# State-space slots: plain fp32 output projection, and the scaled token tile divided between VectorE and GpSimd

## The chip, the core and the metric

One core of a Trainium2 chip runs the whole program. The time is device time of one execution in microseconds (us). The engines are TensorE (PE in the profile, with its weight loads as PEld), VectorE (DVE), ScalarE (ACT), GpSimd (POOL) and SyncE (SP), which here only issues DMAs. They run side by side and wait for one another on semaphores alone.

## What is computed

Two layers on x of shape 2 x 2048 x 256. The first is gated linear attention plus a feed-forward net and a mixture of 14 experts; the second is a state-space block (48 heads of 64 features, state 128) plus a mixture of 16 experts. The change is in the state-space block, whose reference, cut short, is:

```python
proj = _rms(x, norm_w) @ in_proj_w.T
z, xc, B, C, dt = split(proj)
xc = silu(conv_b + sum(conv_w[k] * xp[:, :, k:k + s] for k in range(4)))
dt, A = softplus(dt + dt_bias), -exp(A_log)
def step(h, ins):                       # for each head
    h = exp(A * dt_t) * h + B_t[:, None] * x_t[None, :]
    return h, einsum('np,n->p', h, C_t) + D * x_t
y = _rms(scan(step), inner_norm_w) * silu(z)
out = x + y @ out_proj_w.T
```

## The kernel before

`program` runs stages one after the other: `layer0` (first layer, without its experts), `experts`, `front` (what the second layer needs ahead), `experts1` and `ssm`. The change touches `ssm` and, for the weights that `ssm` reads, `layer0`.

**`ssm`.** Time is cut into G = 8 steps of 512 tokens (4 for each sequence). The 3072 inner features are cut into NCT = 24 tiles of 128, two heads each. A slot g is one tile in one step; N = 192 of them. The state of each tile goes from step to step in `chain`. Each engine runs its own list over the same beats `k`, and works in beat k on slots k to k - 4, so that up to five slots are under way:

- PE: `project(k)` (inputs to x and z, twelve matmuls of split operands), `scores(k-1)`, `update(k-1)` (what the tokens add to the state), `from_state(k-2)`, sometimes `row_turned` (an expert row of the second sequence, slots 6 to 37) and `mean_square`, then `project_out(k-4)` and `turn(k)`, four transposes of x.
- ACT: `convolve`, `output_high(k-4)`, `gate`, `differences`, `tanh`, `square(k-3)`, `decays` and `tokens(k)`, which copies the turned x out of PSUM into `x_tok`.
- POOL: `decayed(k-1)` (two products, tile `mm`), `output_low(k-4)`, `outputs(k-3)` (tiles `y` and `yz`), `squares(k-3)` (`y2`), and, in half of the slots, one small `edge` operation for the start of the convolution.
- DVE: `to_end(k-1)` (tile `xd`, the turned x times its weight up to the end of the chunk), `convolve`, `gate`, `silu`, `scan(k-1)`, `own_tokens(k-1)`, `state_part(k-2)`.

A "split" operand is a pair of tiles, high and low, whose sum is the fp32 value. `mm3` (L60) makes one product of two such pairs in three matmuls; their records have the lines L64, L65 and L66. `yz` is split by `output_high` on ACT (`y_hi`, L2661) and `output_low` on POOL (`y_lo`, L2712), and `project_out` waits for `y_lo`. The weights `wo` come split from HBM, 256 KB a slot.

Order is set by semaphores: `done(engine, name, g)` waits until event `name` has happened for slot g. Once a step, behind its last tile, `mean_square` on PE, `inverse_norm` on ACT (which loads two activation tables) and `evacuate` on DVE finish the step.

**`layer0`.** The weights of `ssm` are split there, tile by tile, between other work: a DMA brings a tile, DVE scales its last 256 columns (`scale_out`, event `s_wo`), ACT copies 768 columns to the high part (L796), POOL subtracts to the low part (L960), and DMAs carry both to `ssm_wi_split` and `ssm_wo_split`.

Of the kernel before, what the change touches and what calls it, by code (L numbers as in the profile page):

```python
# [5 lines left out]
F32 = mybir.dt.float32  # L6
# [7 lines left out]
P = 128  # L14
B, T, D = 2, 2048, 256
KD = D // P
TS = 512
# [82 lines left out]
def program(nc, xT, table, gla_w, gla_wo, wbc, moe0, ffn0, moe1, mamba, a_dram, outT):  # L100
    ctx = ExitStack()
    with ctx:
# [26 lines left out]
        wi_dram = nc.dram_tensor("ssm_wi_split", (NCT, P, 2 * MP_IN), F32, kind="Internal").ap()  # L129
        wo_dram = nc.dram_tensor("ssm_wo_split", (NCT, P, 2 * MP_OUT), F32, kind="Internal").ap()  # L130
        a_drams = (a_dram, nc.dram_tensor("a_scratch1", (HM, T), F32, kind="Internal").ap())
# [115 lines left out]
def layer0(nc, pool, bank, table, tab, vec_dram, xT, gla_w, gla_wo, ffn0, m_dram, ffn_dram, wi_dram, wo_dram, acc_dram, moe0, moe1, down_drams, rows_dram,  # L247
# [11 lines left out]
    with ExitStack() as own:  # L259
# [90 lines left out]
        def done(eng, name, g, per=1):  # L350

            if g >= 0:
                eng.wait_ge(ph[name], (g + 1) * per)
# [39 lines left out]
        with nc.Block(no_gpsimd_drain=True) as block:  # L393

            @block.sync
            def _(sp):
# [22 lines left out]
                def keep(n):  # L419

                    if n is None:
                        return
                    done(sp, "low", n)
                    if n + 1 < SPLITS:
                        fetch(n + 1)
                    if n < NT:
                        sp.dma_start(ffn_dram[n], s_out[:].bitcast(F32)).then_inc(ph["s_kept"], 16)
                    else:
                        parts = s_out[:].bitcast(F32).rearrange("p (h c) -> p h c", h=2)
                        sp.dma_start(wi_dram[n - NT].rearrange("p (h c) -> p h c", h=2), parts[:, :, 0:MP_IN]).then_inc(ph["s_kept"], 16)  # L430
                        sp.dma_start(wo_dram[n - NT].rearrange("p (h c) -> p h c", h=2), parts[:, :, MP_IN:MLP]).then_inc(ph["s_kept"], 16)

# [329 lines left out]
            def _(act):  # L762
# [26 lines left out]
                def high(n):  # L789
                    if n is None:  # L790
                        return
                    split_in(act, n)
                    split_kept(act, n - 1)
                    if n >= NT:
                        done(act, "s_wo", n - NT)
                    act.activation(s_out[:, 0:MLP], s_raw[:, 0:MLP], ACT.Copy).then_inc(ph["high"], 1)  # L796

# [133 lines left out]
            def _(pl):  # L931
# [24 lines left out]
                def low(n):  # L956
                    if n is None:
                        return
                    done(pl, "high", n)
                    pl.tensor_tensor(s_out[:, MLP:2 * MLP], s_raw[:, 0:MLP], s_out[:, 0:MLP].bitcast(F32), ALU.subtract).then_inc(ph["low"], 1)  # L960

# [1374 lines left out]
def ssm(nc, pool, bank, m_dram, wi_dram, wo_dram, a_drams, ea_drams, dec_dram, acc_dram, rows_out, f_dram, outT, st, vec_dram, swdge, tab, col):  # L2336
# [3 lines left out]
    with ExitStack() as own:  # L2340
# [6 lines left out]
        wi = sb("wi", [P, R, 2 * MP_IN], F32R)  # L2347
        wo = sb("wo", [P, R, 2 * MP_OUT], F32R)
        a_wide = sb("a_wide", [P, R, 2, TS])
# [15 lines left out]
        yz = sb("yz", [P, 2, TS])  # L2365
        y_hi, y_lo = sb("y_hi", [P, TS], F32R), sb("y_lo", [P, TS], F32R)
        y2, yr = sb("y2", [P, TS]), sb("yr", [P, TS])
# [40 lines left out]
        with nc.Block(no_gpsimd_drain=True) as block:  # L2408

            @block.sync  # L2410
            def _(sp):
# [17 lines left out]
                def weights_out(g):  # L2429
                    done(sp, "out", g - R)  # L2430
                    sp.dma_start(wo[:, g % R, :].bitcast(F32), wo_dram[g % NCT]).then_inc(ph[f"wo{g % R}"], 16)

# [78 lines left out]
            def _(pe):  # L2511
# [21 lines left out]
                def update(g):  # L2533
                    done(pe, "xd", g)
                    done(pe, "state", g - 1, NJ)
                    for j in range(NJ):
                        i = pe.matmul(bank[:, UPD, chunk(j)], b_tok[:, g // NCT * NJ + j, :], xd[:, j, :],  # L2537
                                      start=True, stop=True)
                    i.then_inc(ph["u"], 1)
# [17 lines left out]
                def project_out(g):  # L2557
                    t, s = g % NCT, g // NCT
                    done(pe, "y_lo", g)
                    landed(pe, "wo", g)  # L2560
                    if t == 0:
                        done(pe, "evac", s - 1)
                    for m in range(KD):
                        a = m * P
                        i = mm3(pe, bank[:, OUT + m, :], (wo[:, g % R, a:a + P], wo[:, g % R, MP_OUT + a:MP_OUT + a + P]),
                                (y_hi[:], y_lo[:]), t == 0, t == LAST)
                    i.then_inc(ph["out"], 1)
# [46 lines left out]
            def _(act):  # L2614
# [42 lines left out]

                def output_high(g):
                    done(act, "yz", g)
                    done(act, "out", g - 1)  # L2660
                    act.activation(y_hi[:], yz[:, g % 2], ACT.Copy).then_inc(ph["y_hi"], 1)  # L2661

                def tokens(g):
                    done(act, "xt", g)
                    done(act, "intra", g - 1)
                    act.activation(x_tok[:].rearrange("p j c -> p (j c)"), bank[:, XT, :], ACT.Copy).then_inc(ph["x_tok"], 1)

# [10 lines left out]
                for k in BEATS:  # L2678
                    if has(k):
                        convolve(k)  # L2680
                    if has(k - 4):
                        output_high(k - 4)
                    if has(k):
                        gate(k)
                        differences(k, 0)
                        tanh(k)
                    if has(k - 3):
                        square(k - 3)
                    if has(k):
                        differences(k, 1)  # L2690
                    e = k - 4
                    if has(e) and e % NCT == LAST:
                        inverse_norm(e // NCT)
                    if has(k):
                        decays(k)
                        tokens(k)

            @block.gpsimd
            def _(pl):
# [8 lines left out]

                def output_low(g):
                    done(pl, "y_hi", g)  # L2710
                    done(pl, "out", g - 1)
                    pl.tensor_tensor(y_lo[:], yz[:, g % 2], y_hi[:].bitcast(F32), ALU.subtract).then_inc(ph["y_lo"], 1)  # L2712

                def outputs(g):
# [6 lines left out]
                    done(pl, "zs", g)  # L2721
                    done(pl, "y_lo", g - 2)
                    pl.tensor_tensor(yz[:, g % 2], y[:], zs[:, g % NS], ALU.mult).then_inc(ph["yz"], 1)  # L2723
# [39 lines left out]
                for k in BEATS:  # L2763
                    if has(k - 1):
                        decayed(k - 1)
                    if has(k - 4):
                        output_low(k - 4)
                    if has(k - 3):
# [9 lines left out]
            def _(dve):  # L2778
# [68 lines left out]
                def to_end(g):  # L2847
                    s, t = g // NCT, g % NCT
                    done(dve, "x_tok", g)
                    done(dve, "u", g - 1)  # L2850
                    dve.tensor_tensor(xd[:].rearrange("p j (h c) -> p j h c", h=2),
                                      bank[:, XT, :].rearrange("p (j h c) -> p j h c", j=NJ, h=2),
                                      w_tok[:, s * NJ:(s + 1) * NJ, 2 * t:2 * t + 2].unsqueeze(3)
                                      .broadcast_to([P, NJ, 2, PH]), ALU.mult).then_inc(ph["xd"], 1)

# [134 lines left out]
```

## Time and profile before

| | |
|---|---|
| time, median of 3 runs | 3035.02 us (3034.8 to 3040.43) |
| profiled execution, span | 3067.1 us, nothing of it lies outside the span |
| PE busy | 2711.5 us, 88% |
| DVE busy | 2384.6 us, 78% |
| ACT busy | 2110.9 us, 69% |
| POOL busy | 1973.4 us, 64% |
| `ssm` | from about 1517 us to the end |

How to read it: the shares are averages over five stages. In the second half of the span, which is `ssm`, each of the four engines is busy for nine tenths or more of nearly every slice; in the first half none but PE is. A matmul's record begins when it starts and ends when its last result is out, so neighbours overlap: what one occupies is the distance to the next start. In the timelines a row stands for several equal instructions in succession (x4), and its second number is from the first start to the last end.

### The profile page before, as it was taken

The numbers are of one execution on the slowest core, as the hardware profiler recorded it, in microseconds if no ns is written. First come the engines' busy times: TensorE is split into PE (matmuls) and PEld (weight loads), VectorE is DVE, ScalarE is ACT, GpSimd is POOL, SyncE is SP. The second block draws the span as 40 slices with busy tenths as digits, with TensorE's granted clock in tenths as the row PEclk, the third lists the DMA queues.
The fourth block names the chain that finished last, engine by engine and source line by source line (L and its number), as shares of the span: only waits on it lengthen the run. The fifth ranks groups of instructions, "written<-read, shape, count | busy, mean of one in ns | idle before, by whom it ended". The sixth has DMA issues, their size and how long they took to land.

```text
span 3067.1 us, 58582 instructions
## 1 busy us (share of the span) xinstructions
PE 2711.5 (88%) x17318; PEld 2120.1 (69%) x17318; DVE 2384.6 (78%) x5972; ACT 2110.9 (69%) x4670; POOL 1973.4 (64%) x1697
## 2 busy tenths in 40 slices
PE   4799999998569888379799999999999999999997
PEld 2466666665469765267588788787887878878786
DVE  3466666666377589558599999998899999999896
ACT  4444454443255466346599999998999999999996
POOL 3322222214424214555399999998999999999998
PEclk7799999997889899689899999999999999999999
DMA  6355445455766544446777776767666666676673
GB/s 168 94 176 170 168 165 185 149 195 168 238 178 199 168 154 151 157 128 199 230 240 237 236 237 205 220 204 220 219 206 217 205 210 216 205 224 199 203 218 113
DMA packets 320436, 588.35 MB, mean 192 GB/s; under 512 B 47888, under 2 KB 138800, under 8 KB 319632
## 3 DMA queue, kind: packets, MB, share of 16 engines
q1 hardware_dynamic: 305776, 545.07, 57.6%
q0 software_dynamic: 14352, 39.54, 3.5%
q8 instruction: 149, 2.44, 0.3%
q14 instruction: 159, 1.30, 0.1%
HBM read 464.44 MB, written 124.17 MB: 192 GB/s over the span
## 4 chain that ended last, share of the span: by engine, by line
POOL 34%; issue 10%; ACT 3%; DVE 1%; PE 1%; DMA 1%; POOLq 1%; SPq 0%; ACTq 0%; DVEq 0%
POOL mm L2706 8%; POOL y L2719 7%; POOL yz L2723 7%; POOL y L2733 6%; POOL y_lo L2712 6%; ACT mt L2636 1%; DVE cv L2789 1%; DMA wi<-ssm_wi_split 1%; POOLq L2382 1%; ACT ys L2650 0%; ACT mt L2656 0%; DVE bank L2860 0%; ACT L2671 0%; POOL first L2748 0%; PE bank L64 0%
## 5 line engine op out<-in xcount | busy, mean ns | idle before, releaser
L2706 POOL TENSOR_TENSOR mm<-mt,cb 128x512 f32<-128x512 f32 x384 | 490.2, 1299 | 56.9 <-ACT mt L2656 54.9
L2636 ACT ACTIVATE mt<-a_wide,a_tok 128x128 f32<-128x128 f32 x1536 | 487.1, 389 | 3.5 <-POOL mm L2706 2.5
L2789 DVE SCALAR_TENSOR_TENSOR cv<-bank,taps,cv 128x509 f32<-128x509 f32 (+2 forms) x576 | 429.3, 745 | 13.6
L64 PE MATMUL bank<-f,wi 128*128 128x512 f32 x768 | 322.4, 420 | 14.7 <-DMA wi<-ssm_wi_split 14.6
L65 PE MATMUL bank<-f,wi 128*128 128x512 f32 x768 | 305.7, 398 | 0.0
L66 PE MATMUL bank<-f,wi 128*128 128x512 f32 x768 | 305.7, 398 | 0.0
L2723 POOL TENSOR_TENSOR yz<-y,zs 128x512 f32<-128x512 f32 x192 | 249.2, 1298 | 15.0
L2712 POOL TENSOR_TENSOR y_lo<-yz,y_hi 128x512 fp32r<-128x512 f32 x192 | 246.2, 1282 | 8.4 <-ACT y_hi L2661 6.5
L2719 POOL TENSOR_TENSOR y<-t 128x512 f32<-128x512 f32 x192 | 246.0, 1281 | 0.0
L2529 PE MATMUL bank<-mm,x_tok 128*64 128x128 f32 x3072 | 226.4, 283 | 13.1 <-POOL mm L2706 13.1
L2733 POOL TENSOR_TENSOR y<-y,ys 128x512 f32<-128x512 f32 x184 | 237.6, 1292 | 0.1
L2529 PEld LDWEIGHTS bank<-mm,x_tok 128*64 128x64 f32 x3072 | 161.4, 136 | 102.9 <-issue 68.1
L2656 ACT ACTIVATE mt<-mt 128x512 f32<-128x512 f32 x384 | 221.4, 624 | 5.9
L2537 PE MATMUL bank<-xd,b_tok 128*128 128x128 f32 x1536 | 223.4, 289 | 0.0
L2537 PEld LDWEIGHTS bank<-xd,b_tok 128*128 128x128 f32 x1536 | 186.7, 192 | 33.1 <-issue 33.1
L960 POOL TENSOR_TENSOR l_s_out<-l_s_raw,l_s_out 128x768 fp32r<-128x768 f32 x33 | 60.5, 1834 | 205.3 <-ACT l_s_out L796 205.3
L2831 DVE SCALAR_TENSOR_TENSOR part<-part,dec,bank 128x64 f32<-128x64 f32 x768 | 181.6, 278 | 13.6
L64 PEld LDWEIGHTS bank<-f,wi 128*128 128x128 f32 x768 | 146.0, 190 | 42.5 <-DMA wi<-ssm_wi_split 15.4
L64 PE MATMUL bank<-y_hi,wo 128*128 128x512 f32 x384 | 171.7, 447 | 3.5 <-POOL y_lo L2712 3.4
L1406 POOL DMA_INDIRECT expert_scratch<-ex_y,ex_home x77 | 73.7, 957 | 150.8 <-ACT ex_y L1495 147.8
L66 PEld LDWEIGHTS bank<-f,wi 128*128 128x128 f32 x768 | 145.6, 190 | 35.8
L65 PEld LDWEIGHTS bank<-f,wi 128*128 128x128 f32 x768 | 146.4, 191 | 26.6
(476 smaller groups left out, 8067.5 us busy)
## 6 DMA issues: line engine op xcount, KB each, us to landing
wi<-ssm_wi_split SPq DMA_DIRECT2D x192, 512.0 KB
a_wide<-a_scratch SPq DMA_DIRECT2D x192, 512.0 KB
l_fw<-ffn_split SPq DMA_DIRECT2D x72, 768.0 KB
ea<-ea_scratch SPq DMA_DIRECT2D x384, 128.0 KB
wo<-ssm_wo_split SPq DMA_DIRECT2D x192, 256.0 KB, 4.1
sorted_scratch<-ex_zeros SPq DMA_DIRECT2D x96, 130.5 KB
ssm_wi_split<-l_s_out SPq DMA_DIRECT2D x24, 512.0 KB
ey_x<-sorted_scratch SPq DMA_DIRECT2D x94, 130.5 KB
```

The lines of the kernel that those rows point to most:

```text
L64: pe.matmul(out, wh, xh, start=first, stop=False)
L65: pe.matmul(out, wh, xl, start=False, stop=False)
L66: return pe.matmul(out, wl, xh, start=False, stop=last)
L2529: i = pe.matmul(bank[h * PH:(h + 1) * PH, INTRA, chunk(j)], x_tok[:, j, h * PH:(h + 1) * PH], mm[:, h, chunk(j)], start=True, stop=True)
L2537: i = pe.matmul(bank[:, UPD, chunk(j)], b_tok[:, g // NCT * NJ + j, :], xd[:, j, :], start=True, stop=True)
L2636: i = act.activation(mt[:, h, chunk(j)], a_wide[:, g % R, h, chunk(j)], ACT.Relu, bias=a_tok[:, s * NJ + j, 2 * t + h:2 * t + h + 1], scal ...
L2706: pl.tensor_tensor(mm[:, :, ts], mt[:, :, ts], cb[:, js, :].rearrange("p j t -> p (j t)") .unsqueeze(1).broadcast_to([P, 2, TS // 2]), ALU ...
L2712: pl.tensor_tensor(y_lo[:], yz[:, g % 2], y_hi[:].bitcast(F32), ALU.subtract).then_inc(ph["y_lo"], 1)
L2719: pl.tensor_tensor(y[:], t1[:], t2[:, g % 2], ALU.add).then_inc(ph["y"], 1)
L2723: pl.tensor_tensor(yz[:, g % 2], y[:], zs[:, g % NS], ALU.mult).then_inc(ph["yz"], 1)
L2733: pl.tensor_tensor(y2[:], y2[:], ys[:], ALU.add).then_inc(ph["y2"], 1)
L2789: dve.scalar_tensor_tensor(cv[:, a:TS], bank[:, X, 0:TS - a], taps[:, t, k:k + 1], cv[:, a:TS], ALU.mult, ALU.add).then_inc(ph["tap"], 1)
```

## The change

Three things. The output projection takes `yz` and `wo` as plain fp32 instead of split: `y_hi`, `y_lo`, `output_high` and `output_low` are gone, and each `mm3` becomes one matmul. The tile `xd` is made in two halves: VectorE makes that of the first head, GpSimd (`second_to_end`) that of the second from `x_tok`, right behind `decayed`; `update` waits for both. In `layer0` the 256 columns of `wo` are only copied, not split.

```diff
@@ layer0, sync
-                        parts = s_out[:].bitcast(F32).rearrange("p (h c) -> p h c", h=2)
-                        sp.dma_start(wi_dram[n - NT].rearrange("p (h c) -> p h c", h=2), parts[:, :, 0:MP_IN]).then_inc(ph["s_kept"], 16)
-                        sp.dma_start(wo_dram[n - NT].rearrange("p (h c) -> p h c", h=2), parts[:, :, MP_IN:MLP]).then_inc(ph["s_kept"], 16)
+                        parts = s_out[:].bitcast(F32)
+                        sp.dma_start(wi_dram[n - NT].rearrange("p (h c) -> p h c", h=2),
+                                     parts.rearrange("p (h c) -> p h c", h=2)[:, :, 0:MP_IN]).then_inc(ph["s_kept"], 16)
+                        sp.dma_start(wo_dram[n - NT], parts[:, MP_IN:MLP]).then_inc(ph["s_kept"], 16)
@@ layer0, scalar
-                    if n >= NT:
-                        done(act, "s_wo", n - NT)
-                    act.activation(s_out[:, 0:MLP], s_raw[:, 0:MLP], ACT.Copy).then_inc(ph["high"], 1)
+                    if n < NT:
+                        act.activation(s_out[:, 0:MLP], s_raw[:, 0:MLP], ACT.Copy).then_inc(ph["high"], 1)
+                        return
+                    act.activation(s_out[:, 0:MP_IN], s_raw[:, 0:MP_IN], ACT.Copy)
+                    done(act, "s_wo", n - NT)
+                    act.activation(s_out[:, MP_IN:MLP].bitcast(F32), s_raw[:, MP_IN:MLP], ACT.Copy).then_inc(ph["high"], 1)
@@ layer0, gpsimd
-                    pl.tensor_tensor(s_out[:, MLP:2 * MLP], s_raw[:, 0:MLP], s_out[:, 0:MLP].bitcast(F32), ALU.subtract).then_inc(ph["low"], 1)
+                    w = MLP if n < NT else MP_IN
+                    pl.tensor_tensor(s_out[:, MLP:MLP + w], s_raw[:, 0:w], s_out[:, 0:w].bitcast(F32), ALU.subtract).then_inc(ph["low"], 1)
@@ ssm
-        wo = sb("wo", [P, R, 2 * MP_OUT], F32R)
+        wo = sb("wo", [P, R, MP_OUT])
-        y_hi, y_lo = sb("y_hi", [P, TS], F32R), sb("y_lo", [P, TS], F32R)
@@ ssm, tensor
                 def update(g):
                     done(pe, "xd", g)
+                    done(pe, "xd1", g)
                     done(pe, "state", g - 1, NJ)
                 def project_out(g):
                     t, s = g % NCT, g // NCT
-                    done(pe, "y_lo", g)
+                    done(pe, "yz", g)
                     landed(pe, "wo", g)
                     if t == 0:
                         done(pe, "evac", s - 1)
                     for m in range(KD):
-                        a = m * P
-                        i = mm3(pe, bank[:, OUT + m, :], (wo[:, g % R, a:a + P], wo[:, g % R, MP_OUT + a:MP_OUT + a + P]),
-                                (y_hi[:], y_lo[:]), t == 0, t == LAST)
+                        i = pe.matmul(bank[:, OUT + m, :], wo[:, g % R, m * P:(m + 1) * P], yz[:, g % 2], start=t == 0, stop=t == LAST)
@@ ssm, scalar
-                def output_high(g):
-                    done(act, "yz", g)
-                    done(act, "out", g - 1)
-                    act.activation(y_hi[:], yz[:, g % 2], ACT.Copy).then_inc(ph["y_hi"], 1)
                 def tokens(g):
                     done(act, "xt", g)
                     done(act, "intra", g - 1)
+                    done(act, "xd1", g - 1)
@@ ssm, gpsimd
-                def output_low(g):
-                    done(pl, "y_hi", g)
-                    done(pl, "out", g - 1)
-                    pl.tensor_tensor(y_lo[:], yz[:, g % 2], y_hi[:].bitcast(F32), ALU.subtract).then_inc(ph["y_lo"], 1)
+                def second_to_end(g):
+                    s, t = g // NCT, g % NCT
+                    done(pl, "x_tok", g)
+                    done(pl, "u", g - 1)
+                    pl.tensor_tensor(xd[:, :, PH:P], x_tok[:, :, PH:P],
+                                     w_tok[:, s * NJ:(s + 1) * NJ, 2 * t + 1:2 * t + 2]
+                                     .broadcast_to([P, NJ, PH]), ALU.mult).then_inc(ph["xd1"], 1)
-                    done(pl, "y_lo", g - 2)
+                    done(pl, "out", g - 2)
@@ ssm, vector
-                    dve.tensor_tensor(xd[:].rearrange("p j (h c) -> p j h c", h=2),
-                                      bank[:, XT, :].rearrange("p (j h c) -> p j h c", j=NJ, h=2),
-                                      w_tok[:, s * NJ:(s + 1) * NJ, 2 * t:2 * t + 2].unsqueeze(3)
-                                      .broadcast_to([P, NJ, 2, PH]), ALU.mult).then_inc(ph["xd"], 1)
+                    dve.tensor_tensor(xd[:, :, 0:PH], bank[:, XT, :].rearrange("p (j c) -> p j c", j=NJ)[:, :, 0:PH],
+                                      w_tok[:, s * NJ:(s + 1) * NJ, 2 * t:2 * t + 1]
+                                      .broadcast_to([P, NJ, PH]), ALU.mult).then_inc(ph["xd"], 1)
```

## Rows read from the trace of the kernel before

**Rows 1.** The profile's page, its first line.
```profile
span 3067.1 us, 58582 instructions
```

**Rows 2.** Busy time: stretch, PE, PEld, DVE, ACT, POOL, then granted clock, DMA.
```profile
2249.00:2289.00 40.00, 40.00 (x289) 33.03 (x286) 36.72 (x78) 37.21 (x90) 39.53 (x32) 1.00 0.66 205
```

**Rows 3.** The page's chain that ended last, by line: share of the span.
```profile
POOL mm L2706 8%; POOL y L2719 7%; POOL yz L2723 7%; POOL y L2733 6%; POOL y_lo L2712 6%; ACT mt L2636 1%; DVE cv L2789 1%; DMA wi<-ssm_wi_split 1%; POOLq L2382 1%; ACT ys L2650 0%; ACT mt L2656 0%; DVE bank L2860 0%; ACT L2671 0%; POOL first L2748 0%; PE bank L64 0%
```

**Rows 4.** Timeline of POOL, a regular slot: start us, us, engine, line, operation.
```profile
2271.68 1.29 POOL L2712 TENSOR_TENSOR y_lo<-yz,y_hi 128x512 fp32r<-128x512 f32 x1
2272.91 1.29 POOL L2719 TENSOR_TENSOR y<-t 128x512 f32<-128x512 f32 x1
...
2279.35 1.28 POOL L2712 TENSOR_TENSOR y_lo<-yz,y_hi 128x512 fp32r<-128x512 f32 x1
```

**Rows 5.** Timeline of PE, the same slot, from turn (L2584) to turn.
```profile
2267.99 0.60 PE L2584 MATMUL bank<-tab,xs 128*128 128x128 f32 x4
...
2271.32 1.12 PE L2529 MATMUL bank<-mm,x_tok 128*64 128x128 f32 x16
2272.36 1.16 PE L2537 MATMUL bank<-xd,b_tok 128*128 128x128 f32 x8
2273.36 0.39 PE L2546 MATMUL bank<-c_feat,chain 128*128 128x128 f32 x2
...
2274.17 0.48 PE L64 MATMUL bank<-y_hi,wo 128*128 128x512 f32 x1
2274.49 0.39 PE L65 MATMUL bank<-y_lo,wo 128*128 128x512 f32 x1
...
2275.42 0.39 PE L66 MATMUL bank<-y_hi,wo 128*128 128x512 f32 x1
2275.65 0.60 PE L2584 MATMUL bank<-tab,xs 128*128 128x128 f32 x4
```

**Rows 6.** Timelines of PE and POOL in slots with an expert row.
```profile
1714.18 0.60 PE L2584 MATMUL bank<-tab,xs 128*128 128x128 f32 x4
...
1722.04 0.60 PE L2584 MATMUL bank<-tab,xs 128*128 128x128 f32 x4
...
1722.40 0.48 PE L64 MATMUL bank<-f,wi 128*128 128x512 f32 x1
...
1722.94 2.59 POOL L2706 TENSOR_TENSOR mm<-mt,cb 128x512 f32<-128x512 f32 x2
...
1726.40 1.16 PE L2537 MATMUL bank<-xd,b_tok 128*128 128x128 f32 x8
```

**Rows 7.** Timeline of PE in `front`: four plain fp32 instructions and what follows.
```profile
1095.80 1.88 PE L1690 MATMUL bank<-fr_acc,tab 128*128 128x512 f32 x4
1097.52 1.04 PE L1716 MATMUL bank<-tab,fr_xn 128*128 128x128 f32 x8
```

**Rows 8.** Timeline of POOL, one edge operation.
```profile
2404.83 0.23 POOL L2748 TENSOR_TENSOR first<-halo,taps 128x12 f32<-128x12 f32 x1
```

**Rows 9.** Line 796, the copy in `layer0`: ns min/median/max; what its engine waited for.
```profile
L796 ACT ACTIVATE l_s_out<-l_s_raw x33: 827/847/852, 20.7 to 664.4; 128x768 fp32r<-128x768 f32 x33
...
  DVE l_s_raw L1219: 73.5, 24
```

**Rows 10.** Timeline of POOL: four of the 25 starts of y in 24 slots.
```profile
2249.92 1.26 POOL L2719 TENSOR_TENSOR y<-t 128x512 f32<-128x512 f32 x1
...
2303.86 1.28 POOL L2719 TENSOR_TENSOR y<-t 128x512 f32<-128x512 f32 x1
...
2331.13 1.33 POOL L2719 TENSOR_TENSOR y<-t 128x512 f32<-128x512 f32 x1
...
2440.11 1.28 POOL L2719 TENSOR_TENSOR y<-t 128x512 f32<-128x512 f32 x1
```

**Rows 11.** Timelines of PE and POOL where a step ends: idle before, releaser.
```profile
2309.12 0.63 PE L2584 MATMUL bank<-tab,xs 128*128 128x128 f32 x4 [0.94 <-ACT yr L2671]
...
2311.59 2.52 POOL L2706 TENSOR_TENSOR mm<-mt,cb 128x512 f32<-128x512 f32 x2 [3.84 <-ACT mt L2656]
```

More of the change, by code:

```diff
@@ L129, in program @@
         wi_dram = nc.dram_tensor("ssm_wi_split", (NCT, P, 2 * MP_IN), F32, kind="Internal").ap()
-        wo_dram = nc.dram_tensor("ssm_wo_split", (NCT, P, 2 * MP_OUT), F32, kind="Internal").ap()
+        wo_dram = nc.dram_tensor("ssm_wo_scaled", (NCT, P, MP_OUT), F32, kind="Internal").ap()
         a_drams = (a_dram, nc.dram_tensor("a_scratch1", (HM, T), F32, kind="Internal").ap())
@@ L2430, in weights_out @@
                     done(sp, "out", g - R)
-                    sp.dma_start(wo[:, g % R, :].bitcast(F32), wo_dram[g % NCT]).then_inc(ph[f"wo{g % R}"], 16)
+                    sp.dma_start(wo[:, g % R, :], wo_dram[g % NCT]).then_inc(ph[f"wo{g % R}"], 16)
                 def inputs(s):
@@ L2680, in _ @@
                         convolve(k)
-                    if has(k - 4):
-                        output_high(k - 4)
                     if has(k):
@@ L2765, in _ @@
                         decayed(k - 1)
-                    if has(k - 4):
-                        output_low(k - 4)
+                        second_to_end(k - 1)
                     if has(k - 3):
```

## The prediction

> **What bounds the kernel now.** I read the page's span first [rows 1], then asked in which stage the change lives. Its loop runs 192 times (8 steps of 512 tokens, 24 pairs of heads each); I call one turn of it a slot. The slots fill about half of the span, so 0.1 us a slot is 19 us, 0.6%. Next comes the table of busy time in a stretch without any special slot [rows 2]: over 40 us PE is busy for 40.00, POOL for 39.53, ACT for 37.21, DVE for 36.72, at a granted clock of 1.00. The chain of waits names POOL lines nearly alone [rows 3]. Reading only that would say that POOL is the bound; the reader should see that PE is just as full, and ask which of the two has the higher floor.
>
> POOL in one regular slot [rows 4]: y_lo, y, yz, y2 and the two halves of mm, back to back, and the next y_lo starts 7.67 us after this one. y_lo takes 1.23 of it, start to start.
>
> PE in the same slot [rows 5]: from turn to turn 7.66 us. Three products with split operands follow one another every (2275.42 - 2274.49) / 4 = 0.2325 us. The pieces: turn and input projection 3.33 us (2267.99 to 2271.32), scores 1.04, update 1.00, from_state 0.81, output projection 1.48. There is no hole in it.
>
> Is 7.66 PE's own floor, or does it follow POOL? The slots that also turn an expert row tell [rows 6]. There are 32 of them (row_turned, slots 6 to 37); PE gets two more transposes, POOL nothing. The period of one is 1722.04 - 1714.18 = 7.86 us, longer than the regular one by 0.20, and two transposes like the turn's four, which occupy 1722.40 - 1722.04 = 0.36 us, are worth 0.18. POOL has ended its mm there (1722.94 + 2.59 = 1725.53) well before PE is through the scores (1726.40). So PE does not follow POOL in this slot: its floor is 7.86 there and some 7.66 elsewhere. PE and POOL are tied within 0.02 us.
>
> **The change part by part.**
> *PE, output projection.* Removed: six matmuls with split operands, 6 x 0.2325 = 1.40 us. (The block spans 1.48 from its first start, but the first record begins 0.08 us before from_state has left the array: from_state's eight instructions take 0.81 there, while the eight of update take 1.00 with 0.1 of entry, so 0.08 belongs to it.) Added: two plain fp32 matmuls of 128x512, which are two instructions each. The same form at the same granted clock, right behind a stream of split products, stands in the stage ahead: four instructions, and the next work of PE starts 1097.52 - 1095.80 = 1.72 us later [rows 7]. So PE gets 1.72 - 1.40 = +0.32 us a slot; +0.24 if the 1.48 is taken instead. I take 0.32, because the 0.08 is made up elsewhere, and keep 0.24 for the low end. PE's slot: 7.66 + 0.32 = 7.98, or 8.18 with an expert row.
>
> Beside this stands a rule of the Trainium skill: "FP8 and Floating Point Precision", TensorE Precision Notes, gives true fp32 four passes through the array. Split products make three. By four passes at 0.2325 the block would take 8 x 0.2325 = 1.86 us, +0.46 a slot. The row disagrees with that: 0.43 us for an instruction is less than two such passes (0.465). The rule points the same way as the row and is a rival below.
>
> *POOL.* Removed: y_lo, 1.23 us. Added: xd1, a 128x256 product. No row has that size; bounds are the 128x12 product of the edge, 0.23 us [rows 8], and the 128x512 ones, 1.28 [rows 4]. Half-way in width lies 0.23 + (1.28 - 0.23) x 244 / 500 = 0.74, which I take. POOL's slot: 7.67 - 1.23 + 0.74 = 7.18 (6.67 to 7.72 from the bounds), and at most 0.2 more where an edge operation runs. All below 7.98: the gain is hidden behind PE.
>
> *ACT* loses y_hi, *DVE* half of xd. Both have slack already, 37.21 and 36.72 of 40 [rows 2]; what they lose brings nothing. Nobody waits for them longer.
>
> *The added wait: update(k-1) on xd1(k-1).* Queued behind it on PE are from_state, the output projection, the turn and the next input projection. PE gets there 1726.40 - 1722.40 = 4.00 us after its input projection started. POOL, now earlier in the slot because it has nothing to catch up on, ended mm 3.13 us after the same moment in the PE-bound slot [rows 6]; plus 0.74 is 3.87. That holds by 0.13 us even without POOL moving forward; with a slot that is 0.32 us longer for PE, ACT and POOL gain that as well. Cost taken: nothing. If xd1 took 1.28, update would start up to 4.41 - 4.00 = 0.41 late without the shift, about 0.1 with it. The wait of the copy into x_tok for xd1 of the slot before, and of yz for the projection two back, end many microseconds before they are asked.
>
> *DMA.* wo comes as 128 KB instead of 256 KB a slot, and nobody waits for it now: nothing.
>
> *The split of the weights in the first layer* (24 tiles). ACT copies 768 columns in 0.85 us, and has waited 73.5 / 24 = 3.1 us before each for VectorE's scaling of the last 256 [rows 9]. Now 512 of them are copied within this wait and only 256 after it, so the tile is done some 0.5 us earlier; at most 24 x 0.5 = -12 us if all of it lay on the path, at worst +24 x 0.2 = +5 for one more instruction. PE is the fullest engine in that stage and hardly waits for these tiles; I take -2.
>
> **The sum.** One step without expert rows has 24 slots in 2440.11 - 2249.92 = 190.19 us [rows 10]. Three of them are special: around the mean square, POOL's y goes from 2303.86 to 2331.13, 27.27 us. In these PE stands idle for 0.94 us before a turn because it waits for ACT's logarithm, and POOL waits 3.84 for the exponentials [rows 11]. The longer projection of that slot disappears in the 0.94; of the other two one gets 0.32; the last, which waits on POOL now, I give 0.1: 27.7. The other 21 slots take (190.19 - 27.27) / 21 = 7.76 on average: POOL's edge operations make half of them longer than 7.67. PE's floor levels them all to 7.98, since POOL's 7.18 + 0.2 stays below it: 21 x 7.98 + 27.7 = 195.3, +5.1 us a step. The 160 slots without expert rows are 6.67 steps: +34. The 32 others get 0.32 each: +10. With the -2: +42 us. Against the profiled execution, 3067.1 us of span with nothing to add around it, that is 3109; the median of the runs is 32 us (1%) below the profiled one, and a difference of 42 scales by nothing that matters: 3035 + 42 = **3077 us**, +1.4%.
>
> **The rivals.**
> (a) *POOL alone sets the slot and PE's fullness is following* (the other side, faster). Then a regular slot goes from 7.76 to about 7.3, 160 x 0.46 = -74, about 2960 us; it decides if PE's 7.86 with an expert row were not a floor. For it: the chain names POOL. Against it: rows 6, and the 1.72 us of [rows 7]. 5%.
> (b) *No change*: half the 0.32 is made up, say by loads of weights that PE no longer waits for (four instead of six), and the edge slots hide the rest: within 6 us of 3035. 4%.
> (c) *update waits for xd1.* If GpSimd's strided product with a broadcast weight costs as much as a full one, PE loses 0.1 to 0.15 a slot on top: 192 x 0.14 = +27, 3104. 12%.
> (d) *Four full passes*, +0.46 a slot: 21 x 8.12 + 27.8 = 198.3, +8.1 a step, 6.67 x 8.1 + 32 x 0.46 = +69, less 2: 3102. It is the time that the page's rule gives. 4%.
> (e) Forecast, 75%: its own range from 0.24 a slot and the whole -12 in the first layer (3035 + 27 - 10 = 3052) to a few tenths lost at the special slots (3090).
>
> **The numbers.** 3077, range 3052 to 3104, which takes in (c) and (d) and leaves out (a) and (b). About 0.2%, 6 us, is what a measurement of this kernel can tell from no change. Faster 0.05, same 0.04, slower 0.91.
>
> **What would show it.** After the change PE should be without a hole in regular slots, with turns 7.98 us apart all along, edge slots and others alike, and 8.18 with expert rows; the projection's four instructions 0.43 apart; POOL idle 0.5 to 0.8 us a slot before mm, waiting for ACT's exponentials; POOL gone from the chain, PE in its place; xd1 near 0.74 us and PE never waiting for it. The forecast is wrong if PE shows idle time before update (then c), or if PE's period in slots without expert rows is below 7.9 (then a or b).

## The result, and the profile after

| | before | after |
|---|---|---|
| median | 3036.2 us, 4 runs (3034.8 to 3040.43) | 3056.98 us, 4 runs (3049.98 to 3059.42) |
| ratio | | 1.0062, 95% interval 1.0046 to 1.0077 |
| PE busy | 2711.5 us, 88% | 2734.9 us, 89% |
| POOL busy | 1973.4 us, 64% | 1840.5 us, 60% |

The change costs 21 us, 0.6%. The forecast was 3077 us: the direction is right and the time lies inside the range, but the forecast size of the change is twice the measured one.

The page of the kernel after, first its span, then two of its groups (busy us, mean ns of one | idle before them, and who ended it):

```profile
span 3057.6 us, 57456 instructions
...
L2703 POOL TENSOR_TENSOR mm<-mt,cb 128x512 f32<-128x512 f32 x384 | 493.2, 1308 | 143.0 <-ACT mt L2659 143.0
...
L2569 PE MATMUL bank<-yz,wo 128*128 128x512 f32 x768 | 363.0, 595 | 0.0
```

POOL now idles 143.0 us ahead of `mm`, 0.74 us for each of the 192 slots in the mean (0.63 in a regular slot; the step ends have more). The new projection is never waited for (0.0). Busy time over 40 us of regular slots, as in [rows 2] (PE, PEld, DVE, ACT, POOL, clock, DMA share, GB/s):

```profile
2209.00:2249.00 40.00, 40.00 (x264) 29.90 (x264) 33.55 (x76) 32.77 (x80) 35.16 (x32) 1.00 0.60 183
```

POOL, 39.53 of 40 in [rows 2], has fallen to 35.16, ACT from 37.21 to 32.77 and DVE from 36.72 to 33.55. PE alone is full. One slot of PE, from turn (L2587) to turn, as [rows 5]:

```profile
2253.56 0.60 PE L2587 MATMUL bank<-tab,xs 128*128 128x128 f32 x4
...
2257.91 1.16 PE L2542 MATMUL bank<-xd,b_tok 128*128 128x128 f32 x8
...
2259.80 1.88 PE L2569 MATMUL bank<-yz,wo 128*128 128x512 f32 x4
2261.51 0.60 PE L2587 MATMUL bank<-tab,xs 128*128 128x128 f32 x4
```

The projection occupies 2261.51 - 2259.80 = 1.71 us, the slot 7.95. From the turn to the projection it is 2259.80 - 2253.56 = 6.24, where [rows 5] have 2274.17 - 2267.99 = 6.18: the 0.06 more is most of the 0.08 that the prediction had given back to from_state. The slots with an edge operation have the same 7.95, and those with an expert row, turn to turn, 1609.53 - 1601.35 = 8.18:

```profile
1601.35 0.60 PE L2587 MATMUL bank<-tab,xs 128*128 128x128 f32 x4
...
1609.53 0.60 PE L2587 MATMUL bank<-tab,xs 128*128 128x128 f32 x4
```

POOL in that regular slot, as [rows 4]:

```profile
2254.11 2.57 POOL L2703 TENSOR_TENSOR mm<-mt,cb 128x512 f32<-128x512 f32 x2 [0.63 <-ACT mt L2659]
2256.65 0.61 POOL L2710 TENSOR_TENSOR xd<-x_tok,w_tok 128x256 f32<-128x256 f32 x1
2257.23 1.27 POOL L2719 TENSOR_TENSOR y<-t 128x512 f32<-128x512 f32 x1
...
2260.17 1.27 POOL L2733 TENSOR_TENSOR y<-y,ys 128x512 f32<-128x512 f32 x1 [0.32 <-ACT ys L2653]
```

`y_lo` is gone, the half of `xd` takes its place for half of the time, and POOL has a hole before `mm` and one before `y2`. The half of `xd` is ready at 2257.26, and `update` starts at 2257.91: the new wait of PE is met 0.65 us early.

**How traces are compared from here on.** The profiled execution of before that the prediction rests on has a span of 3067.1 us against a median of 3035. A second one of the same kernel (e1) had 3038.3. Both spend the same time from the first matmul of `ssm` to the end: 3067.1 - 1509.6 = 1557.5 and 3038.3 - 1481.2 = 1557.1 us. The difference lies ahead of `ssm`, and most of it in `experts1`: from the first to the last start of L2161 it is 1490.1 - 1288.7 = 201.4 us in one trace and 1461.7 - 1283.5 = 178.2 in the other, 23 of the 28 us. Between 1290 and 1380 us the granted clock there was 0.81, 0.89 and 0.77 in three stretches of 30 us, against 0.92, 1.00 and 1.00 in e1 (1285 to 1375); why is not known. So `ssm` is compared by its own distance, against e1, and what is ahead of it on its own. That distance scatters too: e10 has the `ssm` of before unchanged and takes 3027.9 - 1474.6 = 1553.3 us, 4 less than e1, 3.1 of them in the step in which the states are reloaded.

### The profile page after: what moved, and what is told of

Same layout as the page of the kernel before. It is cut to its first block and busy times, and to the rows that moved or that the text cites. A ratio compares the mean times of both kernels' runs of the same rounds, so it can differ in the third digit from the quotient of the medians.

```text
span 3057.6 us, 57456 instructions
## 1 busy us (share of the span) xinstructions
PE 2734.9 (89%) x16934; PEld 2038.2 (67%) x16934; DVE 2324.5 (76%) x5972; ACT 1998.5 (65%) x4502; POOL 1840.5 (60%) x1697
## 3 DMA queue, kind: packets, MB, share of 16 engines
q14 instruction: 156, 1.28, 0.1%
## 5 line engine op out<-in xcount | busy, mean ns | idle before, releaser
L2703 POOL TENSOR_TENSOR mm<-mt,cb 128x512 f32<-128x512 f32 x384 | 493.2, 1308 | 143.0 <-ACT mt L2659 143.0
L2569 PE MATMUL bank<-yz,wo 128*128 128x512 f32 x768 | 363.0, 595 | 0.0
L2719 POOL TENSOR_TENSOR y<-t 128x512 f32<-128x512 f32 x192 | 246.7, 1285 | 0.6 <-DVE t L2844 0.6
L2533 PE MATMUL bank<-mm,x_tok 128*64 128x128 f32 x3072 | 212.1, 279 | 8.8 <-POOL mm L2703 8.8
L2569 PEld LDWEIGHTS bank<-yz,wo 128*128 128x128 f32 x768 | 132.4, 192 | 97.4 <-issue 96.7
L2631 ACT ACTIVATE tz<-bank 128x512 f32<-128x512 f32 x192 | 114.7, 598 | 105.5 <-PE bank L66 105.5
L64 PEld LDWEIGHTS bank<-f,wi 128*128 128x128 f32 x768 | 145.5, 190 | 39.2 <-DMA wi<-ssm_wi_split 13.2
L66 PEld LDWEIGHTS bank<-f,wi 128*128 128x128 f32 x768 | 145.3, 189 | 34.4
L2587 PEld LDWEIGHTS bank<-tab,xs 128*128 128x128 f32 x768 | 95.3, 141 | 108.8 <-issue 102.4
L965 POOL TENSOR_TENSOR l_s_out<-l_s_raw,l_s_out 128x512 fp32r<-128x512 f32 (+1 forms) x33 | 47.4, 1436 | 197.7 <-ACT l_s_out L800 155.0
```

Of the source, the lines that this page charges most:

```text
L64: pe.matmul(out, wh, xh, start=first, stop=False)
L66: return pe.matmul(out, wl, xh, start=False, stop=last)
L2533: i = pe.matmul(bank[h * PH:(h + 1) * PH, INTRA, chunk(j)], x_tok[:, j, h * PH:(h + 1) * PH], mm[:, h, chunk(j)], start=True, stop=True)
L2569: i = pe.matmul(bank[:, OUT + m, :], wo[:, g % R, m * P:(m + 1) * P], yz[:, g % 2], start=t == 0, stop=t == LAST)
L2703: pl.tensor_tensor(mm[:, :, ts], mt[:, :, ts], cb[:, js, :].rearrange("p j t -> p (j t)") .unsqueeze(1).broadcast_to([P, 2, TS // 2]), ALU ...
L2719: pl.tensor_tensor(y[:], t1[:], t2[:, g % 2], ALU.add).then_inc(ph["y"], 1)
```

## The experiments

**Before once more (e1).** No edit; it gives the scatter and the trace that the others are read against.

> The kernel before, unchanged, to see how far its own stages scatter. In the two traces at hand the state-space stage starts at 1509.6 us before and 1472.3 us after, 37 us earlier, and lasts 1557.5 us before and 1585.3 us after (+27.8). The runs differ by only 21. Theory A (the earlier stages scatter from execution to execution, the before trace caught a long one): this trace starts the stage near 1480 us, with a span near 3037, and the stage lasts 1557 again within 1 us. Theory B (the changed weight preparation really shortens the first stages by 30 us or more): the stage starts near 1510 again and the span is near 3067. Ratio to the kernel before: 1.000.

Measured: 3039.1 us, ratio 1.0005 (0.9994 to 1.0016), span 3038.3. The stage starts at 1481.2 us and lasts 1557.1, as theory A had it. Its step end, PE and ACT, answers [rows 11] and is used further down.

**One part at a time (e2, e3).** e2 is after with `xd` whole on VectorE again:

```diff
 def update(g):
     done(pe, "xd", g)
-    done(pe, "xd1", g)
@@ gpsimd
-    def second_to_end(g): ...
@@ vector
-    dve.tensor_tensor(xd[:, :, 0:PH], ...)
+    dve.tensor_tensor(xd[:].rearrange("p j (h c) -> p j h c", h=2), ...)
```

> The kernel after, with the tile xd made whole on VectorE as before, so that only the plain fp32 projection (and its weights) remains. Theory A (PE's own floor of 7.95 us sets every regular slot, xd's place is hidden): PE's period stays 7.95, time within 3 us of the kernel after (3057), ratio 1.006 to 1.008. Rival (the division of xd gave part of the gain that made the result smaller than +42): 5 to 20 us slower than the kernel after, 3062 to 3077.

Measured: 3059.5 us, 1.0068 (1.0053 to 1.0083), the same as the whole change. PE, two turns of a regular slot:

```profile
2253.80 0.60 PE L2586 MATMUL bank<-tab,xs 128*128 128x128 f32 x4
...
2261.75 0.60 PE L2586 MATMUL bank<-tab,xs 128*128 128x128 f32 x4
```

Again 7.95 us; the slots with an edge operation in the middle of a step take 7.95 or 7.96. The whole price of the change is the fp32 projection; within the 2.5 us between the medians, dividing `xd` beside it neither costs nor gives.

e3 is before with the divided `xd` alone (split projection kept):

```diff
 def update(g):
     done(pe, "xd", g)
+    done(pe, "xd1", g)
@@ gpsimd
+    def second_to_end(g): ...   # behind decayed(k - 1)
@@ vector
-    dve.tensor_tensor(xd[:].rearrange("p j (h c) -> p j h c", h=2), ...)
+    dve.tensor_tensor(xd[:, :, 0:PH], ...)
```

> The kernel before, with the tile xd divided between VectorE and GpSimd, and the split projection kept. Theory A (POOL and PE are tied before, so that work added to POOL shows in full): POOL's slot 7.67 + 0.58 = 8.25 us, edge slots 8.4; 160 slots by 0.6 and 32 by 0.45 longer, +105 us, about 3140. Rival (POOL merely follows PE, has slack): no change, 3036 to 3045.

Measured: 3136.9 us, 1.0327 (1.0311 to 1.0342). POOL, its half of `xd` in two successive slots, and 40 us of regular slots:

```profile
2253.26 0.62 POOL L2715 TENSOR_TENSOR xd<-x_tok,w_tok 128x256 f32<-128x256 f32 x1
2253.84 1.28 POOL L2722 TENSOR_TENSOR y_lo<-yz,y_hi 128x512 fp32r<-128x512 f32 x1
...
2261.49 0.62 POOL L2715 TENSOR_TENSOR xd<-x_tok,w_tok 128x256 f32<-128x256 f32 x1
```

```profile
2249.00:2289.00 40.00, 37.83 (x263) 30.29 (x262) 32.31 (x69) 33.90 (x82) 39.38 (x36) 1.00 0.56 184
```

2253.84 - 2253.26 = 0.58 us of POOL more, and the slot is 8.23 instead of 7.67: with `y_lo` still there, POOL pays the half of `xd` in full, 98 us in the sum (105 expected), and PE falls to 37.83. The same 0.6 us that cost nothing in after are the dearest edit of this study in before.

**Is PE the floor after, and POOL the floor before? (e9, e9b)** Both kernels with the output projection cut to little more than half of its work: outside the first and last tile of a step the second matmul takes 64 columns of the 512. What is left out is nearly half of the output projection.

```diff
 def project_out(g):
     for m in range(KD):
+        n = TS if m == 0 or t in (0, LAST) else 64
-        i = pe.matmul(bank[:, OUT + m, :], ..., yz[:, g % 2], ...)
+        i = pe.matmul(bank[:, OUT + m, 0:n], ..., yz[:, g % 2, 0:n], ...)
```

(e9b: the same columns in `mm3`.)

> The kernel after; in every slot the second half of the output projection is made for 64 of its 512 columns only (whole in the first and last tile of a step), so that PE's floor falls evenly in all slots, not in every second one as in the run with even tiles: from 7.95 to 7.95 - 0.86 + 0.11 = 7.20 us. Theory A (the relief of POOL, ScalarE and VectorE was hidden behind PE in full): the slot falls to 7.2 to 7.3, about 2930. Rival (a second limit stands at 7.66, as the mean of the slots with even tiles): about 3003.

> The kernel before with the same part of the output projection left out. PE's floor falls from 7.65 to about 7.65 - 0.70 + 0.3 = 7.2 us in every slot. Theory A (POOL alone holds 7.67, and 7.8 with an edge operation): regular slots stay at 7.67, only the slots with expert rows fall, from 7.86 to 7.67 to 7.8; 3030 to 3036. Rival: below 3000.

Measured: e9 2950.3 us, 0.9706 (0.9686 to 0.9726); e9b 3035.4, 0.9988 (0.9977 to 1.0). First e9, turn, projection and turn of PE, and its stretch; then e9b, a stretch of regular slots, and POOL's `y_lo` in two successive regular slots:

```profile
2255.22 0.61 PE L2588 MATMUL bank<-tab,xs 128*128 128x128 f32 x4
...
2261.59 1.19 PE L2570 MATMUL bank<-yz,wo 128*128 128x512 f32 x4
2262.62 0.60 PE L2588 MATMUL bank<-tab,xs 128*128 128x128 f32 x4
...
2249.00:2289.00 40.00, 39.87 (x284) 31.16 (x284) 38.49 (x93) 35.30 (x86) 37.54 (x34) 1.00 0.73 231
```

```profile
2314.00:2354.00 40.00, 39.05 (x279) 31.87 (x278) 38.56 (x90) 36.93 (x90) 39.49 (x33) 1.00 0.69 229
...
2324.84 1.27 POOL L2713 TENSOR_TENSOR y_lo<-yz,y_hi 128x512 fp32r<-128x512 f32 x1
...
2332.50 1.28 POOL L2713 TENSOR_TENSOR y_lo<-yz,y_hi 128x512 fp32r<-128x512 f32 x1
```

In e9 the projection falls from 1.71 to 2262.62 - 2261.59 = 1.03 us, and the slot from 7.95 to 7.40, the next one to 7.28, which is all of the 0.68 less: PE's time is the slot's time after the change, and 107 us come off. That is between theory A (2930) and its rival (3003), nearer to A: every second slot keeps some 0.1 us. In e9b the projection is shorter by 0.45 us, and the time stays: the regular slot is 2332.50 - 2324.84 = 7.66, POOL's, one with an edge operation has 7.82 as it had before, and PE waits for POOL within the scores of every slot:

```profile
2332.60 0.66 PE L2529 MATMUL bank<-mm,x_tok 128*64 128x128 f32 x8 [0.18 <-POOL mm L2707]
```

So before the change POOL holds the slots when PE is relieved. The other side of the tie, PE's own floor, has no such run, since none relieves POOL alone of as much in before; it rests on [rows 6] and on the slot after the change, where PE alone is full: with the old projection in it, that slot would be 7.95 - 1.71 + 6 x 0.2325 = 7.64 us, against POOL's 7.67.

**Averaging two slots (e5, e6).** To shrink PE's mean load by halves, every second tile's projection was replaced by one narrow matmul; 11 of the 24 output projections of a step are left out (the diff is e6's; e5 takes `y_hi` for `yz`).

```diff
 def project_out(g):
+    if t % 2 and t < LAST:
+        pe.matmul(bank[:, OUT + 1, 0:64], wo[:, g % R, P:2 * P], yz[:, g % 2, 0:64],
+                  start=False, stop=False).then_inc(ph["out"], 1)
+        return
```

> The kernel before; the output projection is made only for the even tiles (and the last) of a step, the odd ones get one matmul of 64 columns: 11 of 24 projections are left out, all else is done. PE's floor falls from 7.65 to about 7.1 us a slot on average. Theory A (before the change POOL holds the slot at 7.67 to 8.1 by itself, tied with PE): regular slots stay at 7.67, only the 32 slots with an expert row get 0.1 to 0.2 shorter; 3028 to 3036. Rival (PE alone holds the slot and POOL follows): 0.5 us a slot, about 2945.

> The kernel after, with the same projections left out. PE's floor falls from 7.95 to about 7.25 on average. Theory A (what the change took off POOL, ScalarE and VectorE is real, but hidden behind PE): the slot follows PE down to its floor or VectorE's, near 7.25, some 0.7 us a slot, about 2930. Rival (another engine or a loop of waits stands right behind PE at 7.9): under 20 us faster than the kernel after, above 3037.

Measured: e5 3035.4 us, 0.9992 (0.9979 to 1.0004); e6 3006.3, 0.9892 (0.9868 to 0.9917). The sign of both fits the tie. The size of e6 met neither of its two expectations: its slots alternate between 6.77 and 8.55 us, 7.66 in the mean. My reading, which no run tests, is that the engines are linked over too few slots for a short one to pay for a long one. That is why e9, which takes the same from every slot, was run.

**The edge operations of POOL, gathered where POOL waits (e7).** If the slots of before with an edge operation are longer only by POOL, moving six of them into the wait behind the mean square ([rows 11], 3.84 us) must shorten before: 1.1 us a step were expected.

```diff
@@ before, gpsimd, half 1
-    if 0 <= t - 1 < 6 and 0 < s < G:
-        edge(s, 1, t - 1)
+    if t == 3 and 0 < s < G:
+        for i in range(6):
+            edge(s, 1, i)
```

> The kernel before, with POOL's six edge operations for the second half of the tiles issued together in the slot of the mean square, where POOL idles 3.8 us for ScalarE, not one each in six slots. Theory A (in edge slots POOL is what holds the slot): five slots a step fall from 7.80 to 7.67 and one from 8.1 to 7.67, 1.1 us a step, for 6 steps -7 us: ratio 0.998. Rival (edge slots are longer for another reason): no change, 1.000.

Measured: 3032.9 us, 0.9981 (0.9968 to 0.9993); `ssm` 1550.4 us against 1557.1. POOL in the gap, then two starts of `y`, and last the same two in e1, where an edge operation lies between them:

```profile
2274.53 0.66 POOL L2748 TENSOR_TENSOR first<-vec,taps 128x36 f32<-128x36 f32 x3
...
2275.88 0.25 POOL L2756 TENSOR_TENSOR first<-first,taps 128x36 f32<-128x36 f32 x1
2278.51 2.53 POOL L2706 TENSOR_TENSOR mm<-mt,cb 128x512 f32<-128x512 f32 x2 [2.37 <-ACT mt L2656]
...
2297.96 1.31 POOL L2719 TENSOR_TENSOR y<-t 128x512 f32<-128x512 f32 x1
2305.68 1.27 POOL L2719 TENSOR_TENSOR y<-t 128x512 f32<-128x512 f32 x1
```

```profile
2302.99 1.31 POOL L2719 TENSOR_TENSOR y<-t 128x512 f32<-128x512 f32 x1
...
2311.12 1.29 POOL L2719 TENSOR_TENSOR y<-t 128x512 f32<-128x512 f32 x1
```

The slot is 7.72 us instead of 8.13, the one before it 7.69 instead of 7.78; the six operations fit into the gap, of which 2.37 us are left. It shows that in before these edge slots were POOL's, with PE waiting. Of the 6.7 us that `ssm` is shorter not all is theirs: 3.4 lie in the step with the reload of the states, which scatters by as much (see e10 above), and the clean steps take 0.8 us less each.

**The copy in the first layer (e4, e10).** e4 is after with the first copy put back behind the wait; e10 is before with nothing but the early copy.

```diff
@@ e4, after, layer0, scalar
+    done(act, "s_wo", n - NT)
     act.activation(s_out[:, 0:MP_IN], s_raw[:, 0:MP_IN], ACT.Copy)
-    done(act, "s_wo", n - NT)
@@ e10, before, layer0, scalar
-    if n >= NT:
-        done(act, "s_wo", n - NT)
-    act.activation(s_out[:, 0:MLP], s_raw[:, 0:MLP], ACT.Copy).then_inc(ph["high"], 1)
+    if n < NT:
+        act.activation(s_out[:, 0:MLP], s_raw[:, 0:MLP], ACT.Copy).then_inc(ph["high"], 1)
+        return
+    act.activation(s_out[:, 0:MP_IN], s_raw[:, 0:MP_IN], ACT.Copy)
+    done(act, "s_wo", n - NT)
+    act.activation(s_out[:, MP_IN:MLP], s_raw[:, MP_IN:MLP], ACT.Copy).then_inc(ph["high"], 1)
```

> The kernel after, with both copies of the weight tile in the first layer behind the wait for VectorE's scaling, as it was before the change. Theory A (the first layer's gain is the earlier copy, a few us): 4 to 8 us slower than the kernel after, 3061 to 3065. Rival (the first layer does not care for it): within 2 us of the kernel after.

> The kernel before with one thing of the change only: in the first layer ScalarE copies the first 512 columns of a weight tile before it waits for VectorE's scaling, and the last 256 after it. Theory A (this is what shortened the stages ahead of the state-space stage by 9 to 12 us): 3025 to 3030, ratio 0.996 to 0.997; the state-space stage starts near 1470, not 1481. Rival (it takes the smaller low part and the smaller transfers of the change too): no change, 3036 to 3038.

Measured: e4 3070.4 us, 1.0111 (1.0093 to 1.0129), 13 us over after where 4 to 8 were expected (9 by the traces); e10 3029.9, 0.9969 (0.9958 to 0.998). The first matmul of `ssm` (first and last start of the line), in this order e1, after, e4, e10:

```profile
L64 PE MATMUL bank<-f,wi x768: 392/398/793, 1481.2 to 3002.9; 128*128 128x512 f32 x192
```

```profile
L64 PE MATMUL bank<-f,wi x768: 393/398/792, 1472.3 to 3024.5; 128*128 128x512 f32 x192
```

```profile
L64 PE MATMUL bank<-f,wi x768: 392/398/793, 1481.1 to 3033.1; 128*128 128x512 f32 x192
```

```profile
L64 PE MATMUL bank<-f,wi x768: 392/398/796, 1474.6 to 2993.5; 128*128 128x512 f32 x192
```

`ssm` begins at 1481 us with the late copy and 7 to 9 us earlier with the early one, in either kernel. Without the first trace of before (1509.6), the six traces with the late copy average 1480.4 and the seven with the early one 1471.0, 9 us; one trace at a time lies up to 8 us off its mean, and the two groups just touch (1476.7 in e9b, 1477.1 in e11). The wait of ACT's copy for VectorE (us, times), first in e1, where the copy is as long as in [rows 9], then in after with the copy behind the wait:

```profile
  DVE l_s_raw L1219: 72.6, 24
```

```profile
L800 ACT ACTIVATE l_s_out<-l_s_raw x24: 416/419/420, 161.3 to 652.7; 128x256 f32<-128x256 f32 x24
...
  DVE l_s_raw L1224: 54.5, 24
```

The stall loses 18.1 us, and what stands behind it is 0.42 instead of 0.85 us long. In e4, where both copies stand behind the wait, it is back at 71.5 us.

**The transfer of `wo` (e8).** In one step PE waits for a tile of `wi` behind the reload of the states. To see whether the halved traffic of `wo` shortens that wait, `wo` was brought with 256 KB again, the second half unused.

```diff
-wo_dram = nc.dram_tensor("ssm_wo_scaled", (NCT, P, MP_OUT), F32, kind="Internal").ap()
+wo_dram = nc.dram_tensor("ssm_wo_scaled", (NCT, P, 2 * MP_OUT), F32, kind="Internal").ap()
...
-wo = sb("wo", [P, R, MP_OUT])
+wo = sb("wo", [P, R, 2 * MP_OUT])
```

> The kernel after, with the plain weight written twice and loaded twice as wide, 256 KB a slot as before, of which the projection uses the first half. Theory A (the volume of wo decides nothing; the one slot in which PE waits for the input weights behind the reload of the states varies by itself): within 2 us of the kernel after, 3055 to 3059. Rival (the smaller load is why that slot took 9.4 us after and 12.5 before): this slot is longer by 3 to 4 us again and the time by as much.

Measured: 3056.0 us, 1.0053 (1.0037 to 1.0069), the same as after. PE's wait (us, times, longest) in e1, in after, and in e8:

```profile
PEld bank L64 <- DMA wi<-ssm_wi_split: 4.7, 1, 4.7
```

```profile
PEld bank L64 <- DMA wi<-ssm_wi_split: 1.4, 1, 1.4
```

```profile
PEld bank L64 <- DMA wi<-ssm_wi_split: 3.4, 1, 3.4
```

The slot is longer again in e8, as the rival had it, but for another reason: the wait is 3.6 in e2 and 1.4 in e4, both with 128 KB, and 3.2 and 2.8 in before and e10, which have the 256 KB of e1. So the volume of `wo` does not set it (e2 and e8 have nearly the same wait with it halved and whole), and it happens once in that step, so that one trace gives one sample. What does set it stays open.

**The two gains together, without the fp32 projection (e11).** e10 and e7 in one kernel.

```diff
@@ before, layer0, scalar
-    act.activation(s_out[:, 0:MLP], s_raw[:, 0:MLP], ACT.Copy).then_inc(ph["high"], 1)
+    act.activation(s_out[:, 0:MP_IN], s_raw[:, 0:MP_IN], ACT.Copy)
+    done(act, "s_wo", n - NT)
+    act.activation(s_out[:, MP_IN:MLP], s_raw[:, MP_IN:MLP], ACT.Copy).then_inc(ph["high"], 1)
@@ before, gpsimd, half 1
-        edge(s, 1, t - 1)
+        for i in range(6):
+            edge(s, 1, i)
```

> The kernel before with the early copy in the first layer and the six edge operations in the gap at the mean square, and with nothing of the plain fp32 projection or the divided tile. If both gains are real and add up: 3036 - 10 - 6 = 3020, ratio 0.995, faster than the kernel before and the kernel after. If the early copy gives nothing: 3030.

Measured: 3022.9 us, 0.9946 (0.9929 to 0.9963), `ssm` 3027.8 - 1477.1 = 1550.7 us. It is the fastest complete kernel of the study: 13 us under before's 3036 (16 under the run beside it) and 34 under after.

## Why the prediction was right or wrong

**Bound and direction: right.** PE and POOL are tied, POOL's side shown by e9b and e3, PE's by [rows 6] and by the 7.64 us worked out above; the new projection lengthens PE, and PE's floor levels all slots, edge slots included (e9). Rival (a), that POOL alone sets the slot, falls by the slot of 7.95 us, and rival (b), no change, by the interval of the ratio. Rival (c), an `update` that waits for `xd1`, falls by the 0.65 us of margin and by e2.

**The projection: right.** Forecast +0.32 us a slot by the four fp32 instructions of [rows 7], measured 1.71 in place of the 1.48 span, 7.95 (forecast 7.98) and 8.18 (8.18) a slot. Rival (d), +0.46 a slot, falls. "FP8 and Floating Point Precision" of the Trainium skill, TensorE Precision Notes, has four passes for true fp32; by an estimate at 0.2325 us a pass, that would be 1.86 us, and the trace has 1.71.

**`xd1`: right where it mattered.** The half takes 0.627 us (median of 192), not 0.74. POOL idles 143.0 / 192 = 0.74 us a slot before `mm`, within the 0.5 to 0.8 announced.

**The chain of waits** was to name PE instead of POOL. It can't be read here: in the trace of after, and in that of e1, it breaks off near the end of the span with 0% everywhere. The holes and the experiments carry the point.

**Where the size failed.** Two terms of the sum were mis-sized: the one for `ssm`, a clean step's +5.1 us times 6.67 and +10 for the expert rows, and the one for the copy in the first layer. The sum had +44 us for `ssm` and -2 ahead of it; measured are +28.3 (1585.3 against 1557.1 in e1) and -9. Taking `ssm` apart by the distances between mean squares (each has 24 output projections), e1 to after, with the forecast's +5.1 a step, or 0.21 a slot:

| | e1 | after | difference | forecast |
|---|---|---|---|---|
| start to first (22 expert rows) | 219.1 | 225.9 | +6.8 | 22 x 0.32 + 2 x 0.21 = +7.5 |
| to the second (10 expert rows) | 190.9 | 196.4 | +5.5 | 10 x 0.32 + 14 x 0.21 = +6.2 |
| third | 190.4 | 194.1 | +3.7 | +5.1 |
| fourth, states reloaded | 195.9 | 195.6 | -0.3 | +5.1 |
| fifth to seventh | 190.4, 190.5, 190.4 | 194.1 each | +3.7, +3.6, +3.7 | +5.1 each |
| last | 178.1 | 179.1 | +1.0 | +5.1 |
| behind the last mean square | 11.4 | 12.0 | +0.6 | 0 |

Within `ssm` three things were off.

1. *Clean steps, +3.7 and not +5.1.* The three special slots were to grow from 27.3 to 27.7. They shrank. Turns of PE around a mean square, e1 and then after, with what ended the idle time:

```profile
2270.64 0.60 PE L2584 MATMUL bank<-tab,xs 128*128 128x128 f32 x4
...
2277.50 1.10 PE L2574 MATMUL bank<-y,tab 128*128 128x512 f32 x2 [0.28 <-DVE xs L2800]
...
2280.97 0.63 PE L2584 MATMUL bank<-tab,xs 128*128 128x128 f32 x4 [0.97 <-ACT yr L2671]
...
2289.90 0.60 PE L2584 MATMUL bank<-tab,xs 128*128 128x128 f32 x4
...
2297.97 0.60 PE L2584 MATMUL bank<-tab,xs 128*128 128x128 f32 x4
```

```profile
2277.42 0.60 PE L2587 MATMUL bank<-tab,xs 128*128 128x128 f32 x4
...
2284.28 1.10 PE L2577 MATMUL bank<-y,tab 128*128 128x512 f32 x2 [0.46 <-DVE xs L2799]
...
2287.26 0.63 PE L2587 MATMUL bank<-tab,xs 128*128 128x128 f32 x4 [0.18 <-ACT yr L2670]
...
2296.52 0.60 PE L2587 MATMUL bank<-tab,xs 128*128 128x128 f32 x4
...
2304.49 0.60 PE L2587 MATMUL bank<-tab,xs 128*128 128x128 f32 x4
```

   Before: 10.33 + 8.93 + 8.07 = 27.33 us. After: 9.84 + 9.26 + 7.97 = 27.07. The wait for the logarithm falls from 0.97 to 0.18: the longer projection takes 0.3 of it, as forecast, and the other half microsecond is that ACT is earlier. ACT at that place, e1 and after:

```profile
2277.02 0.63 ACT L2650 ACTIVATE ys<-y 128x512 f32<-128x512 f32 x1 [0.39 <-POOL y L2719]
...
2278.84 1.28 ACT L2671 ACT_TABLE_LOAD   x1
```

```profile
2283.34 0.61 ACT L2653 ACTIVATE ys<-y 128x512 f32<-128x512 f32 x1
...
2285.14 1.28 ACT L2670 ACT_TABLE_LOAD   x1
```

   Its table load starts 1.34 us behind the mean square in e1 and 0.86 in after; `ys` waited 0.39 us for `y` of POOL in e1 and does not wait now. The prediction had called POOL's gain hidden everywhere; once a step it is not. With the regular slots at 7.95 and not 7.98, 21 x 7.95 + 27.07 - 190.4 = +3.6, which is the measured step. Over four clean steps this is -5.7 us of the 16 that `ssm` missed; the first two miss 0.7 each, presumably in the same way.

2. *The step with the reload, -0.3 and not +5.1.* It was counted as clean. In e1 PE stands 4.7 us for `wi` there and in after 1.4: 3.3 of the 5.4 us. But this difference is mostly luck of the two traces. The same step takes 195.4 us in before, 195.9 in e1 and 192.8 in e10, and 195.6, 195.5, 199.4 and 199.0 in after, e4, e2 and e8: +2.7 in the mean. What makes it scatter is open (e8).

3. *The last step, +1.6 with its tail and not +5.1.* Up to the last turn of PE it grows by 4.1 us (3008.04 - 2848.79 = 159.25 in e1, 3029.87 - 2866.50 = 163.37 in after). Behind that turn there is no input projection any more, PE is not the fullest engine, and the way to the end gets shorter, from 30.3 us (e1; 31.7 in before, 29.3 in e10) to 27.7 (27.6 in e4, 26.8 in e2). In e1 PE stands there for `y_lo`, which after does not have:

```profile
3023.08 0.50 PE L64 MATMUL bank<-y_hi,wo 128*128 128x512 f32 x1 [3.36 <-POOL y_lo L2712]
```

And ahead of `ssm`: the copy brought 9 us, where the bounds were -12 and +5 and I took -2, because "PE is the fullest engine in that stage". By e4 and e10 that was the wrong row to go by: the gain is near the -12 of the bound that puts all of it on the path. Which later work carries it to the end of the stage was not followed.

In sum 28.3 - 9 = +19 against +21 measured by the medians and +42 forecast: 16 us of the miss in `ssm`, 7 in the first layer, less 2 that these two traces don't account for. Over all traces with either program in `ssm` (before, e1, e10 with 1556.0 us in the mean; after, e2, e4, e8 with 1586.9) the stage grows by 31 us, and 31 - 9 = +22 is the measured time.

## What to carry to other kernels

When two engines are both full, find out by slots in which only one has extra work which of them has a floor of its own. A tie charges an addition to either of them in full in every slot where the two are level, while a saving on one brings nothing (e3 +98 us, e9b 0). Where the other engine already takes longer, the addition is partly hidden: the change adds 7.95 - 7.66 = 0.29 us to PE, 56 us in 192 slots, and `ssm` grew by 28, because slots with an edge operation, the end of a step and the drain took part of it up. Price the special slots one by one and don't multiply a clean step by the number of steps: the end of a step, the drain behind the last slot (the work left when no new slot starts) and a step that reloads the states each go their own way. A copy that needs only part of what it waits for is cut in two with the wait in between, and small work belongs into a wait that is there once a step; the two together gave 0.5% where the larger edit lost 0.6%.

## What the runs showed of the hardware

- A plain fp32 product of 128x512 occupies PE for 1.71 / 2 = 0.86 us at the granted clock of 1.00, against 3 x 0.2325 = 0.70 for the split one: 23% more.
- On GpSimd the 128x256 product with a broadcast factor and strides takes 0.627 us (609 to 667), half of the contiguous 128x512 one at 1.28; strides and broadcast cost nothing to be seen. The short 128x36 operation of e7 takes 0.25, hardly over the 0.23 of 128x12 in [rows 8].
- Two traces of one kernel differ by 28 us (0.9%) ahead of `ssm`, and three traces with the same `ssm` (before, e1, e10) by up to 4 us within it, mostly in the one step that waits for `wi`. A stage is compared from its own first instruction.
